# Accumulating scatters in both expert layers, routing that delivers each slot's weight, token mixing in a new order, and a last norm of its own

## The reference, cut to what matters

```python
x = _layernorm(x + _L0_attn_ref(x, ...))   # block-sparse attention, 16 heads
x = _layernorm(x + _L0_ffn_ref(x, ...))    # 8 experts, 2 per token, and a shared MLP
x = _layernorm(x + _L1_attn_ref(x, ...))   # token mixing (a scan) and channel mixing
x = _layernorm(x + _L1_ffn_ref(x, ...))    # 8 experts, 2 per token, capacity 640 each

# _L0_ffn_ref: the gelu experts
moe = jnp.einsum('ted,te->td', y, cw)      # cw: the two weights of each token, else 0
shared = _gelu(xt @ W1) @ W2
return (shared + moe).reshape(B, S, D)

# _L1_attn_ref: EPS 1e-6, _rms(x) = x * rsqrt(mean(x*x) + EPS)
normed = _rms(x); k = normed @ Wk.T; v = normed @ Wv.T; r = sigmoid(normed @ Wr.T)
wkv[t] = state + eu * (k*v)[t];  state = ew * state + (k*v)[t]
x = x + mixer_scale * (r * wkv @ Wo.T)
h = leaky_relu(_rms(x) @ Wfc.T, negative_slope=0.5)
x = x + mlp_scale * (h * h @ Wmlp.T)

# _L1_ffn_ref: the silu experts
y = (routing_w[:, :, None] * sel).sum(axis=1)   # sel: the two expert outputs of a token
```

## Time and profile before

| | |
|---|---|
| median of 3 runs | 2112.03 us (2108.09 to 2112.3) |
| the profiled execution | 2117.18 us, its span 2115.4 us |
| PE busy | 1739.3 us (82% of the span) |
| PEld busy | 1390.0 us (66%) |
| DVE busy | 1202.9 us (57%) |
| ACT busy | 881.9 us (42%) |
| POOL busy | 599.5 us (28%) |
| mean granted TensorE clock | 0.889 |

### The profile page before, as it was taken

The page is one execution under the profiler, slowest core; times in us unless marked ns, Lnnn a source line. Parts: engine busy times, 40 slices in busy tenths (PEclk is TensorE's granted clock), DMA queues, the critical chain, the costliest instruction groups (busy, mean ns, idle before and its releaser), DMA issues. The chain is left out here.

```text
span 2115.4 us, 36910 instructions
## 1 busy us (share of the span) xinstructions
PE 1739.3 (82%) x12492; PEld 1390.0 (66%) x12493; DVE 1202.9 (57%) x2736; ACT 881.9 (42%) x1739; POOL 599.5 (28%) x765
## 2 busy tenths in 40 slices
PE   5759999999994798699999387758887399999970
PEld 4625766666672477577887144457886399999970
DVE  4557677777733766333332488546664655555546
ACT  3200666666682264332232144433442044444336
POOL 1330011111113387423222644122221122312114
PEclk9955899999996599899999699979998599999995
DMA  5694233333303561122222421050001333322206
GB/s 200 245 145 56 53 78 73 76 73 77 75 13 103 172 229 70 50 64 71 64 62 62 142 69 56 0 202 21 21 11 63 100 106 123 108 84 72 77 9 238
DMA packets 142011, 191.00 MB, mean 90 GB/s; under 512 B 70465, under 2 KB 105123, under 8 KB 140864
## 3 DMA queue, kind: packets, MB, share of 16 engines
q1 hardware_dynamic: 113280, 131.79, 20.2%
q0 software_dynamic: 20992, 51.80, 9.0%
q10 hardware_dynamic: 7616, 5.77, 1.5%
HBM read 125.98 MB, written 65.54 MB: 91 GB/s over the span
## 5 line engine op out<-in xcount | busy, mean ns | idle before, releaser
L583 DVE TENSOR_REDUCE att_neg_max<-att_m_ps 128x1 f32<-128x320 f32 x496 | 234.7, 487 | 129.9 <-PE att_m_ps L410 122.3
L410 PE MATMUL att_m_ps<-att_k,att_q 96*128 96x384 f32 x496 | 229.3, 474 | 28.4 <-DMA att_k<-qk 21.0
L1827 PE MATMUL silu_h_ps<-silu_xT,silu_w_part 128*128 128x320 f32 x1536 | 237.9, 312 | 6.4 <-DVE silu_h L1935 3.2
L1827 PEld LDWEIGHTS silu_h_ps<-silu_xT,silu_w_part 128*128 128x128 f32 x1536 | 227.7, 189 | 9.4 <-issue 4.1
L410 PEld LDWEIGHTS att_m_ps<-att_k,att_q 96*128 96x128 f32 x496 | 103.6, 209 | 137.3 <-DVE att_neg_max L583 87.6
L1612 PE MATMUL gelu_y_ps<-layer_wd,gelu_hT 128*128 x576 | 138.0, 382 | 7.8 <-issue 7.1
L548 ACT ACTIVATE att_prob_f<-att_b_ps 128x1024 f32<-128x1024 f32 x64 | 65.6, 1024 | 172.6 <-PE att_b_ps L434 172.6
L2380 PE MATMUL mlp_y_ps<-mlp_wm_part,mlp_h_part 128*128 128x256 f32 x768 | 108.9, 311 | 28.2 <-DVE mlp_h_part L2491 28.2
L2380 PEld LDWEIGHTS mlp_y_ps<-mlp_wm_part,mlp_h_part 128*128 128x128 f32 x768 | 107.3, 220 | 30.4 <-DVE mlp_h_part L2491 30.4
L1573 POOL DMA_INDIRECT gelu_x<-rows,gelu_row_no x72 | 71.7, 996 | 173.7 <-PE gelu_x_ps L1584 156.5
L1612 PEld LDWEIGHTS gelu_y_ps<-layer_wd,gelu_hT 128*128 128x128 f32 x576 | 103.8, 190 | 23.3 <-issue 12.0
(11 more groups left out here) (313 smaller groups left out, 3825.3 us busy)
## 6 DMA issues: line engine op xcount, KB each, us to landing
experts_w<-in_dram SPq DMA_DIRECT2D x24, 1024.0 KB
qk<-qkv_part POOLq DMA_DIRECT2D x32, 512.0 KB, 3.3
att_k<-qk SPq DMA_DIRECT2D x192, 64.0 KB, 2.3
att_q<-qk SPq DMA_DIRECT2D x168, 64.0 KB, 3.0
expert_rows<-gelu_y SPq DMA_DIRECT2D x72, 128.0 KB, 1.7
expert_rows<-mlp_zero SPq DMA_DIRECT2D x8, 1024.0 KB, 16.5
v<-qkv_v POOLq DMA_DIRECT2D x8, 544.0 KB, 4.8
att_v<-v SPq DMA_DIRECT2D x8, 544.0 KB, 4.2
```

What stands on the lines that cost most here:

```text
L410: nc.tensor.matmul(bank[:, 0:2 * LOCAL].rearrange("p (a n) -> p a n", a=2), q[b][0:MROW, x, :], local_and_global(b, x), start=True, stop=T ...
L583: ins = nc.vector.tensor_reduce(neg_max[p % 2][:, x:x + 1], m_ps[u % 2][:, 0:LOCAL + 2 * BLK], AX.X, ALU.max, negate=True)
L1827: mm = nc.tensor.matmul(h_ps[u % 2][a][:, :], w12_part[f % RING][wp][:, a, k, :], xT[s][xp][:, k, rows], start=(i == 0), stop=(i == 3 * KD ...
```

## The change

**Expert results are added in memory.** Neither expert layer stores its results apart. In both, POOL scatters each result tile with `compute_op=ALU.add` straight into the rows of the tokens: `part` (which holds the shared MLP's result) in the first layer, and a new buffer `summed` in the second. A wait for the scatter before stays ahead of each, now in both layers. `expert_rows`, `pos` outside `route`, `gather_pairs`, `add_pairs` and the zero fill are gone. Slots without a token get a row number of 4096, beyond the bound of the scatter. Results must carry their weight, so DVE multiplies as it leaves the bank; there are four result buffers in the first layer (two before) and five in the second.

```diff
-            with pool.Fori(0, NT // XS) as i:
...
-                    nc.gpsimd.tensor_copy(row_no[s][:, :], table[:, bass.ds(n, 1)]).then_inc(numbered, 1)
...
+            def gather(n):
+                s = n % XS
+                if n >= XS:
+                    pool.wait_ge(x_turned, n - XS + 1)
+                nc.gpsimd.indirect_dma_start(out=x[s][:, :], out_offset=None, in_=x_d,
+                                             in_offset=bass.IndirectOffsetOnAxis(ap=table[:, 1, n:n + 1], axis=0)
+                                             ).then_inc(x_in[s], 16)
+
+            for n in range(XS + 2):
+                gather(n)
+            for n in range(NT):
+                if n + XS + 2 < NT:
+                    gather(n + XS + 2)
+                pool.wait_ge(y_ready, n + 1)
+                if n > 0:
+                    pool.wait_ge(y_out, 16 * n)
+                nc.gpsimd.indirect_dma_start(out=sum_d, out_offset=bass.IndirectOffsetOnAxis(ap=table[:, 0, n:n + 1], axis=0),
+                                             in_=y[n % YS][:, :], in_offset=None, bounds_check=T - 1, oob_is_err=False,
+                                             compute_op=ALU.add).then_inc(y_out, 16)
...
-                nc.vector.tensor_copy(y[s][:, :], y_ps[s][:, :]).then_inc(y_ready, 1)
+                if n >= YS:
+                    dve.wait_ge(y_out, 16 * (n - YS + 1))
+                nc.vector.tensor_scalar(y[n % YS][:, :], y_ps[s][:, :], share[:, n:n + 1], None, ALU.mult).then_inc(y_ready, 1)
```

**Routing makes the weights too.** `table_ps` has four columns of tiles in place of one (first layer) or two (second): token number less 4096, the weight cut to fp32r, what that cut leaves, and again the token number, for first and second choices in mirrored order. So each product is three times as wide:

```diff
+    COLS = 4
...
-                nc.vector.tensor_tensor(in_tile[half % HALVES][:, :, :, :], in_tile[half % HALVES][:, :, :, :].bitcast(F32),
-                                        tokens[:, bass.ds(N * q, N)].rearrange("p (t a b) -> p t a b", a=1, b=1).broadcast_to(tiled),
+                spread = [P, 2 * N, COLS - 1, NT]
+                nc.vector.tensor_tensor(in_tile[half % HALVES][:, :, :, :, :].rearrange("p t a c n -> p (t a) c n"),
+                                        is_tile[half % HALVES][:, :, :, :].rearrange("p t (a b) n -> p (t a) b n", b=1).broadcast_to(spread),
+                                        entry[:, N * q:N * (q + 1), :, :].rearrange("p t a (c b) -> p (t a) c b", b=1).broadcast_to(spread),
                                         ALU.mult).then_inc(made, 1)
```

```diff
-                    nc.vector.tensor_tensor(out[s][:, j, :], y_ps[j % 2][:, :],
-                                            x[:, bass.ds(g * GT + j, 1), :].rearrange("p a d -> p (a d)"),
-                                            ALU.add).then_inc(summed, 1)
+                    t = g * GT + j
+                    nc.vector.scalar_tensor_tensor(out[s][:, j, :], y_ps[j % 2][:, :], share[:, t:t + 1], x[:, t, :],
+                                                   ALU.mult, ALU.add).then_inc(summed, 1)
```

**Loops are written out.** Every `Fori` becomes a Python loop, so no engine branches inside a stage:

```diff
-    with eng.Fori(start // 2, NGRP // 2 - 1) as i:
-        step(2 * i, 0)
-        step(2 * i + 1, 1)
-    for g in range(NGRP - 2, NGRP + last):
-        step(g, g % 2)
```

More of the change, by code:

```diff
@@ L114, in _ @@
             src = hsT.rearrange("(k p) t -> p k t", p=P)
-            with sp.Fori(0, NGRP // 2) as i:
+            for i in range(0, NGRP // 2):
                 for s in range(2):
@@ L218, in _ @@
             pool.wait_ge(ones_set, 1)
-            with pool.Fori(0, NGRP) as i:
+            for i in range(0, NGRP):
                 for j in range(4):
@@ L708, in beyond, with skewed @@
     return not isinstance(g, int) or g > n
-def skewed(eng, first, last, step, start=2):
-    for g in range(first, start):
-        step(g, g % 2)
-    with eng.Fori(start // 2, NGRP // 2 - 1) as i:
-        step(2 * i, 0)
-        step(2 * i + 1, 1)
-    for g in range(NGRP - 2, NGRP + last):
+def skewed(first, last, step):
+    for g in range(first, NGRP + last):
         step(g, g % 2)
@@ L911, in step, with last_norm @@
                     norm.copy(act, g - 1, 1 - s)
[L913 to L919, removed]
+            skewed(0, 1, step)
+def last_norm(nc, sum_d, out_d):
     with ExitStack() as ctx:
         m = Mem(nc, ctx, "combine")
[L922 to L927, removed]
-        std, inv, shift = ([m.sb(f"{a}{i}", [P, GT]) for i in range(SETS)] for a in ("std", "inv", "shift"))
+        x = m.sb("x", [P, TT, D])
+        out = m.sb("out", [P, TT, D])
+        part = m.sb("part", [P, TT, 6])
+        mean_var = m.sb("mean_var", [P, TT, 2])
+        std, inv, shift = (m.sb(a, [P, TT]) for a in ("std", "inv", "shift"))
@@ L956, in _ @@
[L956 to L966 removed]
+                sp.dma_start(token_rows(out_d, g), out[:, g * GT:(g + 1) * GT, :]).then_inc(stored, 16)
@@ L1070, in route @@
-def route(nc, tag, xT, Wg, bg, ident, upto, capacity, weight, pos, table, tile_expert, prefetch, shared=None):
+                act.wait_ge(shift_done, g + 1)
+                for t in range(g * GT, (g + 1) * GT):
+                    nc.scalar.activation(out[:, t, :], x[:, t, :], ACT.Identity, bias=shift[:, t:t + 1],
+                                         scale=inv[:, t:t + 1]).then_inc(normed, 1)
+def route(nc, tag, xT, Wg, bg, ident, upto, capacity, table, share, tile_expert, prefetch, shared=None):
@@ L1259, in _ @@
                 step(3, 1)
-                with pe.Fori(2, NGRP // 2) as i:
+                for i in range(2, NGRP // 2):
                     for s in range(2):
@@ L1633, in _ @@
             one(3, 3)
-            with pe.Fori(1, NT // XS - 1) as i:
+            for i in range(1, NT // XS - 1):
                 for s in range(XS):
@@ L1644, in _ @@
                 nc.scalar.copy(wu_part[0][:, k, es, :], wu[:, k, es, :]).then_inc(wu_high, 1)
-            with act.Fori(0, NT // 2) as i:
+            for i in range(0, NT // 2):
                 for s in range(2):
@@ L1680, in _ @@
             take_x(1, 1)
-            with dve.Fori(0, NT // 2 - 1) as i:
+            for i in range(0, NT // 2 - 1):
                 for s in range(2):
@@ L1737, in experts @@
             work(0, 0, True)
-            with eng.Fori(0, E // 2 - 1) as i:
+            for i in range(0, E // 2 - 1):
                 work(2 * i + 1, 1, True)
@@ L1794, in _ @@
             gather(0, 0)
             gather(1, 1)
[L1796 to L1801 removed]
+            for e in range(E):
+                if e + 2 < E:
+                    gather(e + 2, e % 2)
+                scatter(e, e % 2)
             pool.wait_ge(y_out, 16 * NT)
```

810 lines of the change are left out of this document (357 added, 453 removed).

## The result

The changed kernel takes 2098.27 us (2096.71 to 2099.5), beside 2112.16 for the kernel before on the same chip: a ratio of 0.9937, 95% interval 0.992 to 0.9954, so some 13 us less by the ratio (14 by the medians) where 41 were forecast. The profiled execution has a span of 2096.3 us, 19.1 less than that of before.

The account below looks back on a forecast made before the run. It took PE to bound both expert stages and DVE token mixing's steady groups; terms -35 -20 -5 +12 +6 +3 -2 sum to -41, from a median of 2112.0 to 2071 us, range 2045 to 2122.

Parts of the forecast that it names:

- what decides the case: Gelu experts: the step between dependent adding scatters, called the unknown; forecast 3.9 us, beside PE's 3.77 us a tile.
- Gelu experts, the chain: Gelu stage: results leave every 3.9 us in place of 4.0, the last scatter lands later; 5 us less.
- The lower end: Lower bound of the gelu chain's step: a plain scatter's 2.91 to 3.27 us.
- the upper end: Upper bound of the gelu chain's step: a whole read before the write, descriptors once, 4.9 us.
- the middle: Gelu chain's step taken between both bounds, with descriptors and the end message once each: 3.9 us.
- Token mixing: Mixing stage: DVE work removed, groups of 17.5 us bound by PE, earlier start; 35 us less, bounds 22 and 43.
- the chain binds and the kernel is slower: Gelu stage: a scatter step beyond 4.42 us costs more than everything gained; 2149 us at 4.9; chance 0.20.
- First routing: First routing: DVE's third step of a burst writes 1728 elements for 576, taking 3.18 us; 12 us more.
- Second routing: Second routing: DVE sets the pace, with larger steps, wider products and entries; 6 us more.
- Silu experts: Silu stage: PE still sets the pace, five scatters drain one after another at the end; 3 us more.
- Last stage: Last stage: additions leave DVE, weighing leaves ACT, ACT sets the pace at 19.4 us; 20 us less.
- Written-out loops: Loops written out, PE's branch in the gelu experts taking 218 ns 16 times; 2 us less.

Follow-up runs that it names:

- experiment 1: Changed kernel with both expert layers' scatters overwriting rows in place of adding, chain of waits kept: ratio 0.9588 to the kernel before, 74 us less than the changed kernel.
- Experiment 9: Low part of the slots' weights left out in both routings: ratio 0.9888 in the changed kernel, 0.958 in the fastest version.
- experiments 5 and 6: Kernel before, gelu layer: POOL's loop written out, gathers waiting per buffer, index copies between them (0.9918); separately, only PE's loop written out (1.001).
- experiment 6: Kernel before with only PE's loop of the gelu layer written out: ratio 1.001.
- experiment 3: Changed kernel with eight result buffers in place of four in the gelu layer: ratio 0.9918 to the kernel before, 4 us less than the changed kernel.

## Why the prediction was wrong

The measured 2098 lies inside the stated range of 2045 to 2122, but by luck: the gelu stage missed by 60 us one way, and mixing by 24 the other.

- **Right: what decides the case.** The step of the chain was named as the unknown, and the point from which it binds: PE's 3.77 us.
- **Wrong: the term "Gelu experts, the chain", its step of 3.9 us.** It is 4.66 (4.53 in the silu layer). Two steps of its working failed. The lower end was a misread row: of the two plain steps in the earlier trace rows, 3.27 and 2.91, the second belongs to an expert that has hardly any rows. The DMA view of the kernel before shows it, for the five scatters around 1834.04:

```profile
q0 software_dynamic: 225, 0.03, 1.3%
```

  0.03 MB where a full expert sends 0.66. The floor for real data was 3.27, and by the same working the upper end 3.27 + 1.97 = 5.2, the middle 4.25. And the middle itself rested on "descriptors only once, the message once". Descriptors weren't the same: an adding scatter has POOL write for 1.57 us, not 0.97, and its data takes the DMA engines 0.74 us longer (experiment 1). Nothing in the trace of before showed either. By the prediction's own price, 71 results at 4.66 less 3.9, this is 54 us more; the stage came out 60 over its term, the rest being some 3 us each ahead of the first scatter and behind the last.
- **Wrong: the term "Token mixing", -35 for -59**, above its upper bound of 43. The start gave 29 - 12 = 17 for 15. The steady group fell to 15.66, not 17.5: PE's 16.52 was read from a group in which it was idle for 4.5 us; the same group's work is drawn as 15.66 now (the ends of matmuls are modelled, so the difference may be in the drawing). On top came an allowance of 1 for waits, then 8 more for overlap and clock. Eight groups at 21 less 15.66 are 43, and nothing had to be given back.
- **The rival "the chain binds and the kernel is slower"** had the mechanism right: its formula, 77 x step - 340, gives +19 at 4.66. The kernel is faster all the same, because mixing gave 24 more than its term, and both routings and the silu layer 17 more.
- **First routing, +5 for +12.** The third step took 2.49 us, not 3.18: the factor of 1.63 from POOL's work, seen on 576 elements, was 1.28 on 1728 (1.95 undisturbed). Experiment 9 shows how loose such a factor is. Second routing +3 (+4.5 by first instructions) for +6; its step took 2153 ns as foreseen.
- **Silu experts, -4 for +3.** Equal code in this stage differs by up to 7 us between the profiles of the kernel before and of experiments 5 and 6, so nothing can be read from it.
- **Last stage, -21 for -20**: right, by its own steps. ACT is busy 18.76 of the forecast 19.4.
- **Written-out loops.** The -2 was too much already for PE's loop in the gelu layer: experiment 6 has none of it. The other loops weren't tried by themselves. The Trainium skill (Runtime: NRT & Kernel Launch, "Instruction fetch mechanics") says that a taken branch forces a fetch of the target's page before execution goes on if the target isn't in the current two-page window. No run here shows whether this loop's target lies outside it; its 16 branches of PE cost nothing that can be measured.
- The Trainium skill (DMA: Bandwidth & Descriptors, "Latency and other measured facts") gives 0.2 us for an HBM access on average and 2 us at high load. The longer wait measured here, 0.72, lies between, and goes with the data, since it all but vanishes with empty rows. By its lower figure the prediction had a step of 3.1; it is 4.66.

## What to carry to other kernels

A chain of transfers that each wait for the one before costs its step times its length as soon as the step exceeds the pace of the work beside it. More result buffers didn't help here (experiment 3); a second, independent chain did, at once (58 us net, for one more buffer in memory, its zeros and its joining). The releaser that a timeline names is the event that came last, so count tiles before taking it for the cause. When a duration bounds an unknown, look at how many bytes it moved, and when work is added to an engine with slack, look at where in its round the slack lies.

## What the runs showed of the hardware beyond what was expected

- An indirect scatter that adds, 128 rows of 1 KB: POOL writes descriptors for 1.57 us instead of 0.98; 720 packets instead of 240 for five tiles; a dependent step of 4.53 to 4.66 us instead of 3.25. Empty rows: 3.53 instead of 2.90, with as many packets.
- Such a scatter lands 3.8 us after POOL starts it (median), and a scatter that waits for that landing starts 0.85 us later. With two chains, one starts every 3.77 us and still lands after 3.8.
- A POOL addition of 1024 elements (2.4 us) doubled four DVE steps beside it, 2.09 to 4.13 us.
